# A three-layer graph network: two places for kept one-hots, POOL's rows scattered in f32, first one-hots and last node tiles rearranged

## The reference

```python
for k in range(3):
    e = edge_vector @ edge_W[k] + edge_b[k]
    msg = relu(x[src] + e)
    agg = segment_sum(msg, dst, num_segments=n)
    z = (1.0 + eps[k]) * x + agg
    h = relu(batch_norm(z @ W1[k] + b1[k]))      # with stored mean and variance
    x = relu(layer_norm(h @ W2[k] + b2[k], ln_g, ln_b))
return layer_norm(x_in + x)
```

## Time and profile before

| | |
|---|---|
| median of 3 runs | 1654.38 us (1652.43 to 1656.05) |
| profiled execution, its span | 1651.1 us, 1649.3 us |
| busy: PE, weight loads, DVE, ACT, POOL | 1211.7, 978.3, 1214.8, 456.8, 882.0 us |
| DMA | 343.16 MB, 208 GB/s over the span |

### The profile page before, as it was taken

One profiled execution on the slowest core, in us unless ns is written; L12 is line 12 of the kernel. 1 busy time (PEld: TensorE's weight loads), 2 busy tenths in 40 slices (PEclk: granted clock), 3 DMA queues, 4 the chain that ended last, 5 costly groups with the idle time before them and its releaser, 6 DMA issues.

```text
span 1649.3 us, 39429 instructions
## 1 busy us (share of the span) xinstructions
PE 1211.7 (73%) x14458; PEld 978.3 (59%) x14459; DVE 1214.8 (74%) x2181; ACT 456.8 (28%) x846; POOL 882.0 (53%) x842
## 2 busy tenths in 40 slices
PE   2679898898832766775677548898888398898881
PEld 1345444454421765665666447788887387888870
DVE  8766667667655877777877658788887487888886
ACT  0234443443410222222222212233333132333331
POOL 0245556565571754554454057766762477777720
PEclk8799999999975997888788769899999599999995
DMA  5369989889964675555555547788887277877861
GB/s 151 114 225 290 301 284 292 289 287 297 296 224 135 188 210 167 166 181 192 164 170 186 154 121 222 208 236 225 235 237 221 77 223 222 228 234 232 236 164 41
DMA packets 259784, 343.16 MB, mean 208 GB/s; under 512 B 53799, under 2 KB 170585, under 8 KB 259721
## 3 DMA queue, kind: packets, MB, share of 16 engines
q1 hardware_dynamic: 206936, 239.75, 47.1%
q0 software_dynamic: 33280, 82.06, 16.6%
q10 hardware_dynamic: 19505, 20.58, 5.2%
HBM read 229.55 MB, written 112.73 MB: 208 GB/s over the span
## 4 chain that ended last, share of the span: by engine, by line
PE 39%; DMA 29%; DVE 15%; issue 7%; SPq 4%; ACTq 3%; ACT 3%; DVEq 0%
PE ps L1238 18%; DMA region<-kept_dram 13%; DMA kept_dram<-region 8%; DMA rows<-attr_dram 4%; PE ps L1256 4%; DVE hot_stage L914 3%; PE ps L1210 2%; DVE region L958 2%; PE ps L1211 2%; PE ps L1212 2%; PE ps L1213 2%; PE ps L1214 2%; DVE terms L888 2%; DMA xs<-table_dram 2%; ACTq L358 2%
## 5 line engine op out<-in xcount | busy, mean ns | idle before, releaser
L1238 PE MATMUL ps<-xs,region 125*128 125x128 bf16 x5304 | 525.4, 229 | 144.9 <-DVE xs L943 66.9
L555 POOL DMA_INDIRECT rows<-table_dram,src_i x416 | 429.7, 1033 | 245.1 <-issue 119.8
L1238 PEld LDWEIGHTS ps<-xs,region 125*128 125x128 fp8e4 x5304 | 441.1, 101 | 154.2 <-issue 152.7
L1238 PE MATMUL ps<-xr,region 125*128 125x128 bf16 x2652 | 503.7, 229 | 0.0
L540 POOL DMA_INDIRECT srt_dram<-region,pos_i x208 | 234.3, 1126 | 238.0 <-ACT region L612 190.2
L555 POOL DMA_INDIRECT rows<-x_dram,src_i x208 | 215.9, 1038 | 214.3 <-DVE terms L977 161.0
L1238 PEld LDWEIGHTS ps<-xr,region 125*128 125x128 fp8e4 x2652 | 269.0, 101 | 0.0
L620 ACT ACTIVATE terms<-terms 128x512 f32<-128x512 f32 x156 | 97.7, 627 | 375.3 <-DVE terms L970 374.5
L1210 PE MATMUL ps<-wf,rows 128*128 128x384 bf16 x416 | 141.8, 341 | 70.3 <-ACT region L608 51.5
L970 DVE TENSOR_TENSOR terms<-ps,terms 128x512 f32<-128x512 f32 x156 | 106.4, 682 | 71.2 <-PE ps L1238 69.5
L597 ACT ACTIVATE rows<-terms 64x512 bf16<-64x512 bf16 x104 | 81.0, 779 | 270.3 <-DVE terms L888 270.3
(11 more groups left out here) (140 smaller groups left out, 2049.7 us busy)
## 6 DMA issues: line engine op xcount, KB each, us to landing
ep_dram<-terms SPq DMA_DIRECT2D x52, 768.0 KB, 5.1
terms<-srt_dram SPq DMA_DIRECT2D x156, 256.0 KB
terms<-ep_dram SPq DMA_DIRECT2D x156, 256.0 KB
hots<-hotrow_dram SPq DMA_DIRECT2D x156, 208.0 KB
region<-kept_dram SPq DMA_DIRECT2D x26, 562.5 KB
region<-kept_dram SPq DMA_DIRECT2D x26, 546.9 KB
rows<-attr_dram SPq DMA_DIRECT2D x108, 128.0 KB
rows<-attr_dram ACTq DMA_DIRECT2D x100, 128.0 KB
```

What stands on the lines that cost most here:

```text
L555: pool.indirect_dma_start(rows[:, q, t * FEAT:(t + 1) * FEAT], None, source, bass.IndirectOffsetOnAxis(ap=src_i[:, c:c + 1], axis=0),).the ...
L1238: ins = nc.tensor.matmul(bank(q)[:, c:c + FEAT], hot_g[0:SLICE, t // HALF, at:at + P], x_part(part, FIRST[t] + k), start=k == 0 and part == 0,
```

## The change

1. hot_g gets two places, one in early_words (setup arrays that are dead by then), one in region; visit v uses place v % 2. In layer 0 build_hots(j) waits for the store and the gathers of body j - 2. In layers 1 and 2 the load for visit v + 1 is issued in SP's sequence at q = 1 and 3 of visit v's loads.
2. scatter_p takes the f32 rows as they are: one f32 matmul a tile, not three in bf16. The p half of parts goes (L990, L994). The p one-hots are stored as fp8, so the hots of a quad shrink from 832 to 704 bf16 columns, and ACT widens them to f32 (widen, 256 elements a quad) between the two relus, in two places.
3. hots_of runs from body 2 on in the edge stage (g = j - 2), and its last two runs stand in bodies 0 and 1 of layer 0. relT is turned in two pieces, the first between bodies 10 and 11 of the edge stage, the second in layer 0. split_x(0) is done in body 10 of the edge stage, build_hots(0) in body 12.
4. The last four node tiles of a layer run in one round, with PSUM columns and buffers for four. The loads of xs are in two parts: 96 of 125 partition rows after 20 node tiles are stored (table_early), the other 29 after all.
5. PE's layers and bodies and DVE's bodies of layer 0 are written out, not looped.

```diff
+HOT_COLS = QUAD * SORT_WINDOW + QUAD * WINDOW // 2
+EARLY_NODES = 20
+EARLY_ROWS = EARLY_NODES * NODE_TILE // SLICES
+TAIL = 4
...
+        hot_g = [words.bitcast(f8).rearrange("p (h e) -> p h e", h=2) for words in
+                 (early_words[:, hots_words:hots_words + hot_words], region[:, 0:hot_words])]
+        rest_s = region[:, hot_words:hot_words + 2 * QUAD * FEAT].rearrange("p (h e) -> p h e", h=2)
...
+            def load_rel(j, h):
+
+                if j >= 1:
+                    sp.wait_ge(hot_here[(j - 1) % 2][h], 16 * ((j - 1) // 2 + 1))
+                at = j * BLOCK_TILES + h * HALF
+                sp.wait_ge(rel_stored, 16 * (at // P + 1))
...
+            def load_hots(v, h):
+
+                j, before = v % BODIES, v - 2
+                sp.wait_ge(g_filled, before * BLOCK_QUADS + 2 * (h + 1) + BLOCK_QUADS)
+                sp.wait_ge(hot_kept[j % 2][h], 16 * (j // 2 + 1))
+                if before < BODIES:
+                    sp.wait_ge(hot_kept[before % 2][h], 16 * (before // 2 + 1))
+                sp.dma_start(hot_g[v % 2][0:SLICE, h, 0:PAIRS_OF[h] * P],
                              kept[(2 * j + h) * SLICE:(2 * j + h + 1) * SLICE, 0:PAIRS_OF[h] * P]
-                             ).then_inc(hot_here[h], 16)
+                             ).then_inc(hot_here[v % 2][h], 16)
...
+                    load_terms(0, q)
+                load_meta(BODIES - 1)
+                store_hots(BODIES - 3)
+                for v in range(1, VISITS):
+                    l, j = divmod(v, BODIES)
+                    for q in range(BLOCK_QUADS):
+                        h = q // 2
+                        if v < BODIES and q % 2 == 0:
+                            load_rel(v, h)
+                        if v <= BODIES and q % 2 == 0:
+                            keep_hots(v - 1, h)
+                        if BODIES <= v + 1 < VISITS and q % 2 == 1:
+                            load_hots(v + 1, h)
+                        load_terms(v, q)
+                        if l >= 1 and j == 0 and q == 1:
+                            sp.wait_ge(table_early, 16 * EARLY_NODES * l)
                             sp.wait_ge(g_filled, l * LAYER_QUADS + BLOCK_QUADS)
                             for n in range(len(CHUNKS)):
+                                load_slices(sp, tables[l - 1], n, False)
+                    if 1 <= v <= 2:
+                        store_hots(BODIES - 3 + v)
+                    if v == 3:
+                        store_rel(1)
+                    if l >= 1 and j == 0:
+                        sp.wait_ge(table_ready, 16 * (NODE_TILES - EARLY_NODES) * l)
+                        for n in range(len(CHUNKS)):
+                            load_slices(sp, tables[l - 1], n, True)
...
+            def widen(l, j, q):
+
+                wait_alone(act, "act", hots_loaded[q], (l * BODIES + (j + 1)) * 16)
+                wait_alone(act, "act", p_done, l * LAYER_QUADS + j * BLOCK_QUADS + (q + BLOCK_QUADS - 1))
+                nc.scalar.activation(hot_p[:, q % 2, :], hots[:, q, QUAD * SORT_WINDOW:].bitcast(f8),
+                                     ACT.Copy).then_inc(hp_ready, 1)
+
             def relus(l, j, q):
                 relu_s(l, j, q)
+                widen(l, j, q)
                 relu_p(l, j, q)
...
+                if last:
+                    for h in range(TAIL):
+                        scaled(l, NODE_TILES - TAIL + h, h, None)
...
             def build_hots(j, h):
 
-                wait_alone(dve, "dve", relB_loaded[h], (j + 1) * 16)
-                wait_alone(dve, "dve", hot_kept[h], (j + 1) * 16)
-                wait_alone(dve, "dve", g_filled, j * BLOCK_QUADS + 2 * (h + 1))
+                dve.wait_ge(relB_loaded[h], (j + 1) * 16)
+                if j >= 2:
+                    dve.wait_ge(hot_kept[j % 2][h], j // 2 * 16)
+                    dve.wait_ge(g_filled, (j - 2) * BLOCK_QUADS + 2 * (h + 1) + BLOCK_QUADS)
+                elif j == 1:
+                    for q in range(BLOCK_QUADS):
+                        dve.wait_ge(scattered[q], BODIES * 16 * QUAD)
...
             def parts(l, j, q):
 
                 at = quad(l, j, q)
-                whole_s, left_s = terms[:, q, :], rest_s[:, q % 2, :]
-                whole_p, left_p = terms[:, BLOCK_QUADS + q, :], rest_p[:, q % 2, :]
+                whole, left = terms[:, q, :], rest_s[:, q % 2, :]
                 n = QUAD * FEAT
                 dve.wait_ge(s_relu, at + 1)
                 dve.wait_ge(s_done, at + (BLOCK_QUADS - 1))
-                nc.vector.tensor_tensor(left_s, whole_s, high(whole_s, n), ALU.subtract).then_inc(s_rest, 1)
-                dve.wait_ge(p_relu, at + 1)
-                dve.wait_ge(p_done, at + (BLOCK_QUADS - 1))
-                nc.vector.tensor_tensor(left_p, whole_p, high(whole_p, n), ALU.subtract).then_inc(p_rest, 1)
+                nc.vector.tensor_tensor(left, whole, high(whole, n), ALU.subtract).then_inc(s_rest, 1)
                 dve.wait_ge(s_rest, at + 1)
-                nc.vector.tensor_tensor(low(whole_s, n), left_s, high(left_s, n), ALU.subtract).then_inc(s_parts, 1)
-                dve.wait_ge(p_rest, at + 1)
-                nc.vector.tensor_tensor(low(whole_p, n), left_p, high(left_p, n), ALU.subtract).then_inc(p_parts, 1)
+                nc.vector.tensor_tensor(low(whole, n), left, high(left, n), ALU.subtract).then_inc(s_parts, 1)
...
+                    g, q = n // BLOCK_QUADS - 2, n % BLOCK_QUADS
+                    if q == BLOCK_QUADS - 1 and g >= 0:
+                        hots_of(g)
+                        if (g + 1) * BLOCK_TILES == P:
+                            turn_rel(0)
+                    if g == REL_BODY - 3 and q < len(CHUNKS):
+                        split_x(0, [q])
+                    if g == BODIES - 3 and 1 <= q <= 2:
+                        build_hots(0, q - 1)
+
+                def nodes_at_end(l):
+
+                    first = NODE_TILES - TAIL
+                    node_sum(l, first, 0, first, True, tail_zh)
+                    flush(l, BODIES - 1, 0)
+                    node_sum(l, first + 1, 1, first + 1, True, tail_zh)
+                    flush(l, BODIES - 1, 1)
+                    for h in range(2, TAIL):
+                        node_sum(l, first + h, h, first + h, True, tail_zh)
+                    for h in range(TAIL):
+                        node_stats(l, first + h, h, first + h, tail_y)
+                    for h in range(TAIL):
+                        node_norm(l, first + h, h, None, tail_y)
...
             def scatter_p(l, j, q, col):
 
-                pe.wait_ge(p_parts, l * LAYER_QUADS + j * BLOCK_QUADS + (q + 1))
-                whole, left = terms[:, BLOCK_QUADS + q, :], rest_p[:, q % 2, :]
+                v = l * BODIES + j
+                pe.wait_ge(hp_ready, v * BLOCK_QUADS + q + 1)
+                pe.wait_ge(p_relu, v * BLOCK_QUADS + q + 1)
                 for t in range(QUAD):
-                    for part in (high(whole, QUAD * FEAT), high(left, QUAD * FEAT), low(whole, QUAD * FEAT)):
-                        at = QUAD * SORT_WINDOW + t * WINDOW
-                        ins = nc.tensor.matmul(ps[:, bass.ds(col, WINDOW)], part[:, t * FEAT:(t + 1) * FEAT],
-                                               hots[:, q, at:at + WINDOW], start=False, stop=False,
-                                               skip_group_check=True)
+                    ins = nc.tensor.matmul(ps[:, bass.ds(col, WINDOW)],
+                                           terms[:, BLOCK_QUADS + q, t * FEAT:(t + 1) * FEAT],
+                                           hot_p[:, q % 2, t * WINDOW:(t + 1) * WINDOW], start=False, stop=False,
+                                           skip_group_check=True)
                 ins.then_inc(p_done, 1)
...
+                with pe.Fori(0, REL_BODY) as j:
+                    for q in range(BLOCK_QUADS):
+                        staged(j, q)
+                pe.wait_ge(es_taken, REL_BODY * BLOCK_QUADS + 1)
+                turn_rel(0, 3)
+                pe.wait_ge(relT_ready, 1)
+                with pe.Fori(REL_BODY, BODIES) as j:
                     for q in range(BLOCK_QUADS):
                         staged(j, q)
                 pe.wait_ge(es_taken, LAYER_QUADS + 1)
                 pe.wait_ge(ep_taken, LAYER_QUADS + 1)
+                for l in range(LAYERS):
                     gather(l, 0, 0)
                     gather(l, 0, 1)
+                    for j in range(BODIES):
+                        body(l, j)
```

297 lines of the change are left out of this document (147 added, 150 removed).

## The result

The changed kernel takes 1594.12 us (median; 1587.18 to 1595.82), the kernel before 1653.41 in the same runs: ratio 0.9641, 95% interval [0.9597, 0.9684]. Faster, as forecast, but by 59 us instead of 204; 1594 lies outside the range of 1410 to 1500.

The account below looks back on a forecast made before the run. Layer 0 was bound by DVE's waits for stores to kept_dram, with no engine full; POOL was as good as full in layer 2. Terms +18 -55 -97 -9 -26 -9 -18 -8 = -204 gave median 1450; own range 1415 to 1480, 8-in-10 range 1410 to 1500.

Parts of the forecast that it names:

- Edge stage: Stage before the layers: one more hots_of, split_x, build_hots(0) and turning relT add 18 us; bounds +3 and +25.
- gap: Last edge matmul to first scatter: 15.5 us in place of 70.3, -55; bounds 13 and 24.
- Two places: Layer 0: the wait for the store goes; first scatter to last gather takes 290 us, not 387.3; bounds 268 and 335.
- rival A: Layer 0: relB's load, with one place a half, becomes the chain; 28 us a body, 1495 in all; chance 0.12.
- SP issues the hot load ahead of load_terms: Layers 1 and 2: loading one-hots first queues nothing behind it; DMA share about 0.83 at 21 us a body.
- The late 29 rows should land in 5: Layer ends: late xs rows land 5 us after the tables; gather(0,2) starts 16.8 after them instead of 22.
- f32 scatter: scatter_p: four f32 matmuls replace 12 bf16; 0.61 us a quad for 0.36, +1.0 a body, +13 a layer.
- rival C: scatter_p: the f32 matmuls cost 0.98 us a quad, +1.5 a body more; 1496 in all; chance 0.12.
- Rival E: scatter_p: f32 matmuls run as in the tail, 9.5 us a body for 1.4; 1727 in all; chance 0.02.
- Rival B: All layers: POOL paces, 285 us in layers 1 and 2, 8 more in layer 0; 1468 in all; chance 0.12.
- Rival D: Layer 0: two places don't part store from build, the 32 us body stays; +97, 1547 in all; chance 0.03.
- two signs of being wrong: Layer 0's loop settles above 26 us a body, or f32 weights don't load behind the matmul before.

Follow-up runs that it names:

- c_after: The control: the changed kernel itself, unchanged, run again beside e5, e6_all and e7; 1604.77 us, 0.9718 of the kernel before.
- e5: Changed kernel with relB's loads moved ahead of the terms loads in SyncE's order; 1570.76 us, 0.9498 of the kernel before.
- e7: e6_all with the f32 scatter undone (three bf16 matmuls again, VectorE makes the parts of both halves); 1505.31 us, 0.9112 of the kernel before.
- e6_all: Changed kernel with 32 late xs rows, relB and gather one-hots on 128 rows, relB's loads moved forward; 1471.18 us, 0.8901 of the kernel before.

## Why the prediction was wrong, by its own steps

- **Edge stage** (+18) and **gap** (-55): right, +17.8 and -52. That the edge stage hit within 0.2 is partly luck: its last matmul starts at 487.8 here, at 489.1 in c_after, the same program, and at 477.4 to 487.3 in the other three of that group, whose edge stage differs little. **The end**: -11 for -8.
- **"Two places", layer 0, 290 with bounds 268 and 335**: 363, the largest miss. The step that failed is "what is late next is the sum of each engine's own work". What was late next was rival A's loop, which had a chance of 0.12. Its mechanism was right and its sum was not. "14.6 + L" left out the node normalisation and x_eps between build and gather(2) (4.2 us) and the transposition (1.2); it took gather(2) at 3.2 us instead of 5.38, the scatters, clears and hidden layer at 3.9 instead of 4.7, and SyncE's issues at 1.8 instead of 0.9. That makes 22 + L; with the measured L of 7.83 it is the measured 29.8, where A's own sum gives 22.4. So A was priced as harmless below L = 9.4. That A's price of 28 us a body is the measured mean, 363.4/13 = 28.0, is chance, since it stood on an L of 13.5. Without the waits for relB (e5) 36 of the 73 us went.
- **"SP issues the hot load ahead of load_terms ... nothing is queued behind it"; DMA at "about 0.83 ... below the 0.9"**: this failed in layers 1 and 2. The share is a mean over sixteen engines, 0.76 and 0.78 after, and hides the five that carry the one-hots; terms loads behind them landed after 13 us, and VectorE waited 154.8 us for them. From gather(0,2) layer 1 took 294 us (923.75 to 1217.9), layer 2 282 (1268.97 to 1551.0), forecast 263.
- **"The late 29 rows should land in 5"**: 18 us after issue in layer 1's end. gather(0,2) began 30.2 and 22.8 us after the tables instead of 16.8, 19 us in all. Layer ends before that: 24.2 and 28.3 for 22 and 22.4.
- **f32 scatter, 0.61 a quad**: 0.89, eight records 0.11 apart, 0.09 short of rival C's 0.98 and close to the 0.85 that the prediction estimated from the Trainium skill (TensorE: Matmul & The Clock Gate, LDWEIGHTS (loading the stationary operand)). The step "the f32 load may lie behind the matmul before it" failed: on PE the edit costs +2.1 us a body, not +1.0, so 14.6 us a layer more than forecast. Rival E did not happen: 0.11 a record, not 0.6.
- **widen at nothing**: right as far as seen; it waited 32.8 us in 36 times for the scatter two quads back, and nobody's long wait is for it.
- **Rival B** (POOL paces): not in the kernel after; it appeared in e7, at the 20 us a body to which PE then fell.
- **Rival D**: no; the waits on kept_dram are gone from layer 0, and PE's in layer 2 as well.
- **The prediction's two signs of being wrong** both came: bodies of layer 0 above 26 us (28 to 33), and f32 records 0.11 apart, where it named 0.06 to 0.08, and 0.12 for C.

With relB's loads moved forward and the narrow transfers spread, e6_all takes 1471 us, 21 above the forecast of 1450 and inside its range: the forecast's engine sums held within that, and its transfers did not. Part of this is luck. From gather(0,2) on PE was to be busy 245.3 + 13 = 258 us a layer and is busy 261.3 and 262.6 in e6: of the 14.6 us that f32 costs beyond the forecast, some 10 are made up by the rest of PE's work, at a granted clock of 1.00 and 0.99 where the forecast's 245.3 us had 0.97.

## What to carry to other kernels

Before a wait is removed by more buffers, ask why the transfer behind it is slow: in this kernel a DMA's rows sat on one or five engines of sixteen, and the mean DMA share did not show it. Look at what share of the engines one queue holds while a lone transfer runs. Here 128 rows for 125 and 32 for 29 took it away. A loop through a single-place buffer is to be summed from every piece of the chain of one body, low-clock matmuls and the issuing queue's order included, before its landing time is called harmless.

## What the runs showed of the hardware that was not expected

- Rows and engines: 29 rows 5.6% of sixteen engines (one) at 0.14 MB in 6.2 us, 125 rows 27.4% (five) at 0.62 MB in 5.6 us, 32 rows with others 38.8%.
- Behind narrow transfers in its queue an issue can itself take long: the p terms' has a median of 0.50 us and a longest of 4.8 in the control, a median of 0.32 in e6, whose longest (5.1) stand behind 93 rows.
- Two kinds of chip: the same program 1654 or 1883 to 1889 us, the first gathers at about the same time, PE's matmuls in the layers in batches 0.73 or 1.43 us apart on the slower kind; VectorE's and GpSimd's instructions have the same lengths on both (the add of terms 0.69 us on both, a gather 1.05 and 1.00).
- With less idle time on PE the granted clock was higher as well: in layer 0 it went from 0.86 to 0.96 as half of PE's 70 idle us went away (34 in e6), and gather(2), 5.38 us in the chain of the kernel after, took 3.09 in most of e6's bodies.
